# A graph kernel's edge sort moved from the front of the program into layer 1's blocks, as a check

## The chip, the cores and the metric

The kernel runs on one core of one Trainium2 chip. The metric is the device time in microseconds (us), the median of the runs. "PE" is TensorE, "DVE" VectorE, "ACT" ScalarE, "POOL" GpSimd, "SP" SyncE, which here only issues transfers.

## The reference

Two layers of a graph network over N = 6250 nodes and E = 206250 edges, width 64, all in float32. The edges are 100000 random pairs in both directions and a self-loop per node, sorted by `dst`.

```python
h = relu(layernorm(x))
# layer 0: edge (row, col) = (src, dst); 4 heads
e = concat(h[row], h[col])                            # 128 wide
a = pos[col] * exp(lrelu(lrelu(e @ gate_w1.T) @ gate_w2.T))
b = lrelu(lrelu(e @ msg_w1.T) @ msg_w2.T)
x = x + mean_heads(segment_sum(a * b, row) / segment_sum(a, row))
h = relu(layernorm(x))
# layer 1: gathers from src, sums at dst
m = (h[src] * sigmoid(feat @ prob_w.T)
     + (feat @ review_w.T) * sigmoid(feat @ score_w.T) * weight) * cj[src]
x = x + segment_sum(m, dst) * ci
```

Layer 0 sums at `src`, layer 1 at `dst`, while the input is sorted by `dst`.

## The kernel before

The edges stand in 403 blocks of 512 (4 tiles of 128), four blocks being a quad; the last one is partly padding. Both layers go block by block, and in both the sorted end of a block's edges lies in a narrow window of node numbers, so its rows come as a product with a 0/1 matrix, while the other end is gathered by indirect DMA.

The stages, in order of time:

- *Norm and tables* (VectorE L1189 to L1206). Then a loop over 49 columns of nodes builds `window_table`, the nodes' rows times the first weights in a high and a low part: PE `turn_column`, `project`, `project_rest`; ScalarE `copy_column`, `copy_high`, `copy_low` (L996 to L1016); GpSimd copies two small tail columns (L784); SP writes the rows out (L555, L558). After the loop ScalarE's queue issues the writes of `split_table`, the gather table of layer 0 (L1033, L1034), and the zeroing of the sums (L888).
- *The sort.* Layer 0 needs the edges by `src`. VectorE makes keys (`src` and `dst` packed in one positive float) and sorts all of them by a bitonic network: each of 128 partitions holds a run of 2048, a pass compares elements at a distance (`sort_pass`, L1429 and, for the passes after a turn, L1426), and between passes over runs and over partitions the array is transposed by PE in four PSUM banks (L1989), with ScalarE and VectorE moving two banks each (L1042, L1045, L1502, L1504). Then the sorted list is unpacked (`by_src`, `by_src_dst`, `by_src_first`), stored to DRAM, and each block's first node loaded back.
- *The verdict.* From the offsets of both lists a number `fits_sb` is made (L1566, L1569): 1 where each block's window is narrow enough. All engines load it (`fits`) and branch: `If` is the way with windows, `Else` a general way for any edge list, which isn't run with these inputs.
- *Layer 0* (`edges0_windows` on each engine, in loops of four blocks). SP loads a block's 32 rows of the window table (L535), the list's row (L540) and the gather's indices (`load_index`, L527). GpSimd gathers the far rows (L751, four a block) and adds the sums to DRAM (L765). PE is the busiest engine.
- *Between the layers* the sums are divided, added to `x`, normed again, and `src_table` is stored.
- *Layer 1* (`edges1_windows`, in loops of eight blocks). GpSimd gathers the `src` rows (L853, four a block, in four buffers; the gather of a block waits for the terms of the block four back). VectorE makes two dots (L1701, L1707), the 0/1 columns (L1733), and from the gathered rows the terms (L1737 to L1745). PE sums a quad in one bank (L2038), projects and adds it.

The order of the work is written out by hand for each engine; semaphores join them. In layer 1 of VectorE the part around the change is this:

```python
nc.vector.tensor_tensor(hot_four[m], columns_ps..., offset..., ALU.is_equal).then_inc(hot_ready, 1)   # L1733
dve.wait_ge(gates_ready, b + 1)
nc.vector.tensor_tensor(feat_gate_ps, gates_ps[:, 1, :], attn_quads[odd][:, m, :], ALU.mult)...       # L1737
dve.wait_ge(gathered1w[m], 64 * (quad + 1))
nc.vector.tensor_tensor(terms1_windows[m][:, :, 0:D], ends1_windows[m][:, :, 0:D], gates_ps...)       # L1739
```

Tiles whose names end in `_ps` are in PSUM.

## Time and profile before

| | us |
|---|---|
| median of 3 runs | 6826.49 (6826.26 to 6827.18) |
| span of the profiled execution | 5851.6 |
| its own time | not given beside the span |
| table build (36 to 176) | 140 |
| rest of the sort, verdict (176 to 522) | 346 |
| layer 0 (522 to 3795) | 3273 |
| between the layers (3795 to 3832) | 37 |
| layer 1 (3832 to 5852) | 2020 |

The span is the time from the first to the last instruction in the record; the median is 974.9 us longer. An engine's busy time counts its instructions, not its waits. A transfer stands in the record of the queue that issues it (SPq, ACTq) with the time of the issue alone, and as a share of the 16 DMA engines. The stretches' bounds are read off the timeline: the first window load of layer 0 and the first full blocks of layer 1.

### The profile page before, as it was taken

What the parts mean: (1) busy time and instruction counts of PE and PEld (TensorE: products, weight loads), DVE (VectorE), ACT (ScalarE), POOL (GpSimd) and SP (SyncE); (2) the same over time, 40 slices, a digit from 0 to 9 for tenths busy, and PEclk for the clock granted to TensorE, in tenths of its full rate; (3) what the DMA queues carried; (4) which work ended last, traced back from release to release, by engine and by line L of the source; (5) the groups of instructions that cost most, each with busy time, mean ns of one, the idle gap of its engine ahead of it and who ended that gap; (6) DMA issues with size and microseconds to landing.
All of it is one profiled execution on the core that took longest, in us unless ns stands there. A gap on an engine that the chain in (4) does not pass through costs nothing.

```text
span 5851.6 us, 116285 instructions
## 1 busy us (share of the span) xinstructions
PE 4355.2 (74%) x25010; PEld 2801.2 (48%) x25010; DVE 4656.5 (80%) x10137; ACT 2612.7 (45%) x6383; POOL 3496.4 (60%) x3689
## 2 busy tenths in 40 slices
PE   6214999999999999999999999545555555455455
PEld 4212555555555555555555555334444444444444
DVE  9887988989889898988989889756666666666665
ACT  5102777777777777777777777510000000000000
POOL 1002656666565665656656566367777777777776
PEclk9656999999999999999999999855555555555555
DMA  6601333333333333333333333333333323322332
GB/s 247 130 0 47 78 79 80 77 80 79 78 81 78 78 80 78 81 78 78 81 78 80 79 78 80 97 73 59 56 56 56 59 56 56 60 56 56 60 56 51
DMA packets 459109, 437.02 MB, mean 75 GB/s; under 512 B 268369, under 2 KB 340274, under 8 KB 457906
## 3 DMA queue, kind: packets, MB, share of 16 engines
q0 software_dynamic: 122512, 173.81, 18.0%
q1 hardware_dynamic: 308706, 249.41, 15.3%
q10 hardware_dynamic: 27840, 13.23, 1.4%
q8 instruction: 18, 0.29, 0.0%
q14 instruction: 33, 0.27, 0.0%
HBM read 363.27 MB, written 72.83 MB: 75 GB/s over the span
## 4 chain that ended last, share of the span: by engine, by line
PE 46%; POOL 17%; issue 13%; DVE 12%; DMA 6%; ACT 4%; ACTq 1%; SPq 0%; POOLq 0%; DVEq 0%
PE ps_hidden L1814 9%; POOL work L853 9%; PE ps_beta L1866 9%; POOL ends L853 8%; PE ps_hidden L1815 7%; PE ps_beta L1874 7%; DMA ends<-src_table,src_quads 5%; PE ps_alpha L1848 4%; DVE work L1429 4%; DVE work L1317 4%; PE ps_sum L1885 3%; ACT beta_scaled L949 3%; PE ps_T L1803 3%; PE ps_alpha L1857 2%; DVE work L1739 1%
## 5 line engine op out<-in xcount | busy, mean ns | idle before, releaser
L751 POOL DMA_INDIRECT ends<-split_table,src_pairs x1612 | 1581.0, 981 | 1571.7 <-issue 1435.0
L1317 DVE TENSOR_TENSOR work<-work,ps_hidden 128x512 f32<-128x512 f32 x1612 | 1102.3, 684 | 25.4 <-ACT work L897 6.5
L1814 PE MATMUL ps_hidden<-ends_parts,w_high 128*128 128x512 f32 x2418 | 1064.4, 440 | 60.5 <-DVE work L1317 58.8
L897 ACT ACTIVATE work<-ps_hidden 128x512 f32<-128x512 f32 x1612 | 960.6, 603 | 63.2 <-PE ps_hidden L1815 34.6
L1815 PE MATMUL ps_hidden<-ends_hot,window 128*128 128x512 f32 x2418 | 953.4, 394 | 0.0
L853 POOL DMA_INDIRECT work<-src_table,src_quads x808 | 764.4, 946 | 309.2 <-issue 222.0
L853 POOL DMA_INDIRECT ends<-src_table,src_quads x804 | 760.5, 946 | 245.2 <-issue 226.0
L2038 PE MATMUL ps_beta<-work,dst_rows_sb 128*128 128x128 f32 x1608 | 416.4, 441 | 565.6 <-DVE work L1745 565.6
L1115 ACT ACTIVATE ps_alpha<-dots 128x8 f32<-128x8 f32 x403 | 72.7, 180 | 1676.4 <-DVE dots L1707 1676.4
L1866 PE MATMUL ps_beta<-work,msg_w_sb 128*64 128x512 f32 x3224 | 804.1, 609 | 0.4 <-DVE work L1317 0.2
L2038 PE MATMUL ps_beta<-work,equal 128*128 128x128 f32 x1616 | 417.2, 440 | 509.1 <-DVE work L1745 509.1
L1322 DVE TENSOR_TENSOR beta<-beta_scaled,ps_beta 128x512 f32<-128x512 f32 x806 | 552.2, 685 | 288.1 <-ACT beta_scaled L949 280.3
L949 ACT ACTIVATE beta_scaled<-ps_beta 128x512 f32<-128x512 f32 x806 | 488.0, 605 | 562.1 <-PE ps_beta L1866 562.1
L1814 PEld LDWEIGHTS ps_hidden<-ends_parts,w_high 128*128 128x128 f32 x2418 | 454.6, 188 | 580.0 <-DVE work L1317 517.5
L2038 PEld LDWEIGHTS ps_beta<-work,dst_rows_sb 128*128 128x128 f32 x1608 | 358.1, 328 | 639.6 <-issue 611.1
L2038 PEld LDWEIGHTS ps_beta<-work,equal 128*128 128x128 f32 x1616 | 359.8, 328 | 556.1 <-issue 451.3
L897 ACT ACTIVATE scaled<-ps_hidden 128x512 f32<-128x512 f32 x806 | 489.6, 607 | 250.4 <-PE ps_hidden L1815 197.3
L1317 DVE TENSOR_TENSOR work<-scaled,ps_hidden 128x512 f32<-128x512 f32 x806 | 547.7, 679 | 2.3 <-ACT scaled L897 2.3
L1874 PE MATMUL ps_beta<-ident,beta 128*128 128x128 f32 x3224 | 506.4, 280 | 0.8 <-DVE beta L1322 0.7
L1815 PEld LDWEIGHTS ps_hidden<-ends_hot,window 128*128 128x128 f32 x2418 | 457.3, 189 | 56.2
L1874 PEld LDWEIGHTS ps_beta<-ident,beta 128*128 128x128 f32 x3224 | 357.1, 141 | 167.6 <-issue 165.6
L765 POOL DMA_DIRECT2D sums<-key_rows x403 | 371.3, 921 | 64.1 <-issue 28.4
(204 smaller groups left out, 6650.2 us busy)
## 6 DMA issues: line engine op xcount, KB each, us to landing
window<-window_table SPq DMA_DIRECT2D x403, 192.5 KB
parts<-in_edge_attr SPq DMA_DIRECT2D x101, 512.0 KB
dst_rows_sb<-by_src SPq DMA_DIRECT2D x403, 128.0 KB
ends<-split_table,src_pairs POOLq DMA_INDIRECT x1612
window_table<-parts SPq DMA_DIRECT2D x49, 386.0 KB, 2.4
sums<-key_rows POOLq DMA_DIRECT2D x403, 32.6 KB
work<-src_table,src_quads POOLq DMA_INDIRECT x808, 2.5
ends<-src_table,src_quads POOLq DMA_INDIRECT x804, 2.5
```

The lines of the kernel that those rows point to most:

```text
L751: pool.indirect_dma_start(out=ends[m][:, t, :], out_offset=None, in_=split_table, in_offset=bass.IndirectOffsetOnAxis(ap=src_pairs[m // 2] ...
L765: pool.dma_start(sums0[0][bass.ds(first, WIN0), :], quad_sum[m * WIN0:(m + 1) * WIN0, :], accum_op=ALU.add).then_inc(quad_added, 16)
L853: pool.indirect_dma_start(out=ends1_windows[m][:, t, :], out_offset=None, in_=src_table, in_offset=bass.IndirectOffsetOnAxis(ap=src_quads[ ...
L897: nc.scalar.activation(scaled[k % NL][:, :], ps_hidden[k % NL][:, :], ACT.Copy, scale=SLOPE).then_inc(scaled_ready, 1)
L949: nc.scalar.activation(beta_scaled[:, a * B:(a + 1) * B], ps_beta[a][:, :], ACT.Copy, scale=SLOPE).then_inc(beta_scaled_ready, 1)
L1317: nc.vector.tensor_tensor(hidden[k][:, :], scaled[k % NL][:, :], ps_hidden[k % NL][:, :], ALU.max).then_inc(hidden_ready, 1)
L1322: nc.vector.tensor_tensor(beta_T[a], beta_scaled[:, a * B:(a + 1) * B], ps_beta[a][:, :], ALU.max).then_inc(beta_ready, 1)
L1814: nc.tensor.matmul(o, w1_high[:, k * P:(k + 1) * P], ends_parts[j][:, :], start=True, stop=False)
L1815: nc.tensor.matmul(o, window[j][:, k * P:(k + 1) * P], ends_hot[j][:, :], start=False, stop=True).then_inc(hidden_done, 1)
L1866: last = nc.tensor.matmul(ps_beta[a][i * D:(i + 1) * D, :], msg_w2_sb[:, 2 * a + i, :], hidden[2 + 2 * a + i][:, :], start=True, stop=True)
L1874: last = nc.tensor.transpose(ps_beta[a][:, t * P:(t + 1) * P], beta_T[a][:, t * P:(t + 1) * P], ident[:, :])
L2038: last = nc.tensor.matmul(ps_beta[odd][0:WIN, 0:W1], hot_four[m][:, t, :], terms1_windows[m][:, t, :], start=(m == 0 and t == 0), stop=(m ...
```

## The change

Since the edges are given in both directions, the list by `src` is the list by `dst` with its ends swapped. Layer 0 now takes the input's list: `dst` as the sorted end where the sum goes, `src` as the gathered one. The exact check that this is right for the given edges is a sort of signed keys: an edge's key is its two ends packed (smaller first), with the sign of `src - dst`, 0 for self-loops and padding. The sorted keys, reversed and added to themselves, must be 0 everywhere. This sort runs in layer 1, from block 10 on, half a pass in a block of VectorE, half a turn in a block of PE and ScalarE. The verdict comes after layer 1. If it is 1 there is nothing more to do; `Else` starts again from `x` and computes both layers in the general way.

The core of the diff; `wait_more` and `begin_again` are of the `Else` way alone.

```diff
 # the plan, worked out while the program is built
+        def sort_plan():
+            halves, rounds, of, steps, moved, turn, b = {}, {}, 0, 1, 0, 0, SORT_FROM      # SORT_FROM = 10
+            def two_halves(d, run, turned, length):
+                for half in range(2):
+                    halves[b + half] = (of, d, run, turned, length, half, steps, moved)
+                return 1 - of, steps + (2 if run is None else 4), b + 2
+            for k in range(1, RUN_BITS + 1):                                               # RUN_BITS = 11
+                for i in range(k - 1, -1, -1):
+                    of, steps, b = two_halves(1 << i, (1 << k) if k < RUN_BITS else None, False, kept(1 << k))
+            for k in range(RUN_BITS + 1, SORT_BITS + 1):                                   # SORT_BITS = 18
+                for inward in (True, False):
+                    for r in range(2):
+                        rounds[b + r] = (turn, 2 * r, of, None if inward or k == SORT_BITS else k - RUN_BITS, steps)
+                    of, turn, moved, b = 1 - of, turn + 1, 4 * turn + 4, b + 2
+                    for i in range(k - RUN_BITS - 1, -1, -1) if inward else range(RUN_BITS - 1, -1, -1):
+                        run = (1 << (k - RUN_BITS)) if inward and k < SORT_BITS else None
+                        of, steps, b = two_halves(1 << i, run, inward and i == k - RUN_BITS - 1, RUN)
+            return halves, rounds, of, steps, turn, b
+        HALVES, ROUNDS, SORTED, SORT_STEPS, TURNS, MIRROR = sort_plan()
+        SETTLE = MIRROR + 6
 # VectorE
+            def sort_half(of, d, run, turned, length, half, steps, moved):
+                wait(dve, sort_moved, moved)
+                dve.wait_ge(sort_step, steps)
+                if run is None:       # one instruction of 1024 elements
+                    order_pairs(pairs(1 - of, d)[half], pairs(of, d), turned, (ALU.min, ALU.max)[half])
+                else:                 # two of 512
+                    out, given = pairs_of_way(1 - of, d, run, half, length), pairs_of_way(of, d, run, half, length)
+                    order_pairs(out[half], given, turned, ALU.min)
+                    order_pairs(out[1 - half], given, turned, ALU.max)
+            def check_part(b):
+                if SORT_FROM - 4 <= b < SORT_FROM:
+                    key_part(b - SORT_FROM + 4)      # one to four instructions of 1616 elements
+                if b in HALVES:
+                    sort_half(*HALVES[b])
+                if 0 <= b - MIRROR - 2 < 4:
+                    mirror_part(b - MIRROR - 2)      # 512 sums of a turned bank and the keys reversed
+                if 0 <= b - SETTLE < 8:
+                    settle_part(b - SETTLE)          # reach and mirror sums into fits_sb
             def edges1_windows(b, quad, half, m, odd):
...
                 nc.vector.tensor_tensor(hot_four[m], columns_ps...).then_inc(hot_ready, 1)
+                check_part(b)
                 dve.wait_ge(gates_ready, b + 1)
...
-            with dve.If(fit):
-                quads(dve, edges1_windows)
+            every_block(edges1_windows)             # written out; so are PE's and ScalarE's
+            fit = fits(dve)
+            with dve.If(fit):
+                settle(dve)
 # PE, ahead of a block's sums
+            def turn_round(n, i, of):
+                wait(pe, sort_moved, 4 * n + i)
+                for c in range(4):
+                    last = nc.tensor.transpose(turn_bank[:, c * P:(c + 1) * P],
+                                               runs[of][:, (4 * i + c) * P:(4 * i + c + 1) * P], ident[:, :])
+                last.then_inc(sort_turned, 1)
             def edges1_windows(b, quad, half, m, odd):
+                if b in ROUNDS:
+                    turn_rounds(*ROUNDS[b])          # two rounds
+                if 0 <= b - MIRROR < 6:
+                    mirror_rounds(b - MIRROR)
                 pe.wait_ge(terms1_step, 4 * b + 4)
 # ScalarE, behind a block's gates
+                if b in ROUNDS:
+                    move_rounds(*ROUNDS[b])          # each: wait sort_turned, copy the bank to the other run
 # ScalarE, start: the writes of the gather table ahead of the loop
             copy_high(0)
+            act.wait_ge(parts_split, 2)
+            act.wait_ge(step, STEPS_TABLE0)
+            act.dma_start(nodes(split_table)[:, :, 0:D], h_parts[0]).then_inc(tables_split, 16)
+            act.dma_start(nodes(split_table)[:, :, D:2 * D + 1], table_sb[:, :, :]).then_inc(tables_split, 16)
             for t in range(NT):
                 copy_low(t)
...
-            act.wait_ge(parts_split, 2)
-            act.wait_ge(step, STEPS_TABLE0)
-            act.dma_start(...)                       # the same two
             act.wait_ge(zeros_set, 1)
             zero_sums0(0, zeroed)
 # SP
             def load_index(b, a):
-                sp.dma_start(src_pairs[a][:, :], by_src_dst[:, bass.ds(b * T, 2 * T)]).then_inc(index_in[a], 16)
+                sp.dma_start(src_pairs[a][:, :].rearrange("p (b t) -> p b t", t=T),
+                             src[bass.ds(b, 2)].rearrange("b p t -> p b t")).then_inc(index_in[a], 16)
                 sp.dma_start(dst_rows_sb[j][D:P, :, :],
-                             by_src[bass.ds(b, 1)].broadcast_to([P - D, T, P])).then_inc(window_in[j], 16)
+                             dst_rows[bass.ds(b, 1)].broadcast_to([P - D, T, P])).then_inc(window_in[j], 16)
 # GpSimd
+            pool.wait_ge(tables_split, 32)
+            for b in range(3):
+                gather0_windows(b, 0, b)
+                gather0_tiles(b, T // 2)
+            pool.wait_ge(fits_step, 3)
+            pool.wait_ge(zeroed, 16 * 5)
+            fours(pool, edges0_windows)
 # VectorE during the table loop: the tail copies (GpSimd's before), the split of the far
 # weights, the offsets of both windows and their reach
+            for t in range(NT):
+                tail_rows(t)
+                if t == 1:
+                    split_far_weights()
...
```

After layer 0's sums are in, SP loads `src` and `dst` again for the keys, 1616 numbers a partition, behind the stores of `src_table`. The sort's two arrays now lie in `centered` and `table_sb`, the signs and the mirror's sums in `x_sb`.

## Rows read from the trace of the kernel before

**Rows 1.** The page: the span; busy us of each engine and share.

```profile
span 5851.6 us, 116285 instructions
PE 4355.2 (74%) x25010; PEld 2801.2 (48%) x25010; DVE 4656.5 (80%) x10137; ACT 2612.7 (45%) x6383; POOL 3496.4 (60%) x3689
```

**Rows 2.** By stretch: busy us of each engine, clock, DMA share, GB/s.

```profile
36.00:176.00 140.00, 118.75 (x687) 88.79 (x686) 137.85 (x230) 89.14 (x245) 20.18 (x47) 1.00 0.73 274
176.00:240.00 64.00, 7.32 (x32) 6.55 (x32) 45.93 (x42) 2.46 (x4) 0.00 (x0) 0.50 1.09 163
240.00:522.00 282.00, 49.77 (x211) 43.20 (x211) 247.76 (x280) 15.24 (x24) 0.00 (x0) 0.51 0.02 7
522.00:3795.00 3273.00, 3155.33 (x20150) 1795.31 (x20150) 2917.85 (x5693) 2355.50 (x5423) 1949.11 (x2015) 0.99 0.37 80
3795.00:3832.00 37.00, 1.56 (x7) 1.56 (x8) 21.23 (x49) 19.30 (x78) 8.33 (x9) 0.50 0.44 162
3832.00:5852.00 2020.00, 1021.12 (x3924) 865.30 (x3923) 1255.43 (x3815) 127.77 (x603) 1516.64 (x1604) 0.50 0.30 56
```

**Rows 3.** Groups of lines: busy us, mean ns, idle before; VectorE.

```profile
L1429 DVE TENSOR_TENSOR work<-work 128x512 f32<-128x512 f32 (+5 forms) x450 | 366.3, 868 | 5.8
```

**Rows 4.** Groups by form in layer 1, 4200 to 5600 us.

```profile
L853 POOL DMA_INDIRECT ends<-src_table,src_quads x560 | 529.7, 946 | 170.8 <-issue 158.3 <-DVE ps_sum L1742 6.4 <-DMA attn_quads<-in_edge_weight 4.9
L1739 DVE TENSOR_TENSOR work<-ends,ps_alpha 128x256 f32<-128x256 f32 x140 | 59.0, 421 | 251.0 <-DMA ends<-src_table,src_quads 251.0
L1739 DVE TENSOR_TENSOR work<-work,ps_alpha 128x256 f32<-128x256 f32 x140 | 59.0, 421 | 247.7 <-DMA work<-src_table,src_quads 247.7
```

**Rows 5.** Timeline, verdict to first block: start us, us, engine, line.

```profile
521.79 0.14 DVE L1569 TENSOR_SCALAR fits_sb<-reach 1x1 int32<-1x1 f32 x1
...
523.83 0.52 SPq L535 DMA_DIRECT2D window<-window_table  x1
...
527.99 0.49 DVE L1306 TENSOR_SCALAR ends_hot<-dst_rows_sb,window 64x512 fp32r<-64x512 int32 x1 [6.06 <-DMA dst_rows_sb<-by_src]
```

**Rows 6.** Timelines of SP's and ScalarE's queues, table's end.

```profile
175.73 0.33 SPq L558 DMA_DIRECT2D window_table<-parts  x1
...
175.25 0.62 ACTq L1033 DMA_DIRECT2D split_table<-parts  x1
...
175.90 13.64 ACTq L1034 DMA_DIRECT2D split_table<-table_sb  x1
189.59 23.96 ACTq L888 DMA_DIRECT2D sums<-parts  x5
```

**Rows 7.** By stretch, as rows 2, after the split_table issues.

```profile
189.60:218.00 28.40, 3.65 (x16) 3.27 (x16) 12.12 (x13) 1.09 (x2) 0.00 (x0) 0.50 1.29 95
218.00:232.00 14.00, 3.67 (x16) 3.27 (x16) 12.48 (x13) 1.37 (x2) 0.00 (x0) 0.50 0.99 413
```

**Rows 8.** Groups by form, 100 to 560 us: the sort.

```profile
L1429 DVE TENSOR_TENSOR work<-work 128x1024 f32<-128x1024 f32 x170 | 200.7, 1222 | 3.4
L1429 DVE TENSOR_TENSOR work<-work 128x512 f32<-128x512 f32 x168 | 105.0, 687 | 1.5
```

**Rows 9.** Timeline: a turn of the sort, three banks of four.

```profile
378.56 2.82 PE L1989 MATMUL ps_hidden<-ident,work 128*128 128x128 f32 x12 [27.26 <-DVE work L1429]
```

**Rows 10.** GpSimd's small copy: ns min/median/max, first and last start.

```profile
L784 POOL COPY parts<-tails x49: 188/418/694, 35.2 to 172.9; 128x4 f32<-128x4 f32 x49
```

**Rows 11.** Timelines of GpSimd and VectorE in layer 0, in order.

```profile
2000.51 1.05 POOL L751 DMA_INDIRECT ends<-split_table,src_pairs  x1 [0.30 <-issue]
...
2004.71 1.06 POOL L751 DMA_INDIRECT ends<-split_table,src_pairs  x1 [0.82 <-DVE parts L1330]
...
2005.00 0.28 DVE L1348 TENSOR_TENSOR equal<-columns,src_offset 128x128 fp32r<-128x128 f32 x1
...
2013.64 0.94 POOL L751 DMA_INDIRECT ends<-split_table,src_pairs  x1 [3.59 <-issue]
...
2013.98 0.28 DVE L1348 TENSOR_TENSOR equal<-columns,src_offset 128x128 fp32r<-128x128 f32 x1
```

More of the change, by code:

```diff
@@ L579, in _ @@
-            with sp.Else():
-                sp.wait_ge(lists_stored, 48)
-                blocks(sp, load0)
-                sp.wait_ge(zeroed1, 16 * T)
-            def read_sums0(c, copies):
-                if c >= 2 and copies == 1:
-                    sp.wait_ge(part_free, c - 1)
-                elif c >= 2:
-                    sp.wait_ge(x_summed, 2 * (c - 1))
-                for t in range(copies):
-                    sp.dma_start(parts[c % 2][:, t, :, :],
-                                 nodes(sums0[t][0:NP, :])[:, c * CH:(c + 1) * CH, :]).then_inc(part_in[c % 2], 16)
+            sp.wait_ge(fits_step, 3)
@@ L1390, in _ @@
-            for k in range(7):
-                nc.vector.tensor_scalar(lane[:, k:k + 1], lane[:, k:k + 1], k, 1, ALU.logical_shift_right,
-                                        ALU.bitwise_and).then_inc(signs_step, 1)
-            dve.wait_ge(signs_step, 7)
-            nc.vector.tensor_scalar(signs[:, 0:7], lane[:, 0:7], -2.0, 1.0, ALU.mult, ALU.add).then_inc(signs_step, 1)
-            keys = runs[1].bitcast(I32)
-            nc.vector.scalar_tensor_tensor(out=keys[:, 0:LIST], in0=runs[0][:, 0:LIST].bitcast(I32), scalar=FIELD,
-                                           in1=keys[:, 0:LIST], op0=ALU.logical_shift_left,
-                                           op1=ALU.bitwise_or).then_inc(key_step, 1)
@@ L1441, in offsets_of_targets, with tail_rows, split_far_weights @@
-            def offsets_of_targets():
+            dve.wait_ge(tail_step, 2)
+            def tail_rows(t):
+                if t >= 2:
+                    dve.wait_ge(row_out[t % 2], 16 * (t // 2))
+                nc.vector.tensor_copy(low_row[t % 2].rearrange("p (a w) -> p a w", a=2)[:, :, 0:2],
+                                      tails[:, t, :, :]).then_inc(tail_ready, 1)
+            def split_far_weights():
+                dve.wait_ge(w_high_ready, 1)
+                for j in range(2):
+                    nc.vector.tensor_tensor(window[j][0:D, 0:HID], w1_far[0:D, :], w1_high[0:D, :].bitcast(F32),
+                                            ALU.subtract).then_inc(w_low_ready, 1)
@@ new lines, in signs_of_lanes, with offsets_of_quads @@
+            def signs_of_lanes():
+                dve.wait_ge(lanes_ready, 1)
+                for k in range(7):
+                    nc.vector.tensor_scalar(lane[:, k:k + 1], lane[:, k:k + 1], k, 1, ALU.logical_shift_right,
+                                            ALU.bitwise_and).then_inc(signs_step, 1)
+                dve.wait_ge(signs_step, 7)
+                nc.vector.tensor_scalar(signs[:, 0:7], lane[:, 0:7], -2.0, 1.0, ALU.mult, ALU.add).then_inc(signs_step, 1)
+            def offsets_of_quads():
@@ L1509, in _ @@
-            for k in range(1, RUN_BITS + 1):
-                for i in range(k - 1, -1, -1):
-                    at = sort_pass(at, 1 << i, (1 << k) if k < RUN_BITS else None, length=kept(1 << k))
-            for n, (k, inward, _, _) in enumerate(TURNS[:-1]):
-                at = turn_runs(n, k, inward, at)
-                for i in passes(k, inward):
-                    run = (1 << (k - RUN_BITS)) if inward and k < SORT_BITS else None
-                    at = sort_pass(at, 1 << i, run, turned=inward and i == k - RUN_BITS - 1)
@@ L2078, in project_sums @@
                 last.then_inc(review_done, 1)
+            fit = fits(pe)
             with pe.If(fit):
-                quads(pe, edges1_windows)
-                turn_window(NQ - 1)
-                project_window(NQ - 1)
+                settle(pe)
             with pe.Else():
+                begin_again(pe)
+                transpose_ends(0, 0, 0)
+                blocks(pe, edges0)
+                for t in range(T):
+                    sum_tile(NB - 1, t, 1)
                 blocks(pe, edges1)
```

1039 lines of the change are left out of this document (520 added, 519 removed).

## The prediction

> **What bounds the kernel now.** I read the busy table first, then a table by stretches, then in each stretch the groups of lines and a timeline, always with one question: which engine never waits here.
>
> The span is 5851.6 us [rows 1]. The page gives no other time of the profiled execution; the median of the runs is 6826.5, so 974.9 us lie around the span. Nothing in the trace shows what they are. I hold them fixed: every sum below is taken from the span and carried over as it stands.
>
> The stretches are the key [rows 2]. From 36 to 176 us the window table is built: PE and ACT work, the DMA share is 0.73, VectorE is busy 138 of 140 us, but with the sort, not with the table. From 176 to 522 only VectorE works: PE is busy 57 of 346 us and GpSimd not at all. The sort's line L1429 has 450 instructions of 366.3 us [rows 3]. This part is serial: nothing of layer 0 starts before the sorted list. Layer 0 (522 to 3795) has PE busy 3155 of 3273 us at clock 0.99, 8.1 us for each of 403 blocks. Layer 1 (3832 to 5852) is different: PE 1021, VectorE 1255 and GpSimd 1517 of 2020 us, 5.0 us a block. There the gathers bound it: each takes 0.946 us, 170.8 us of idle time stand before 560 of them, 0.30 us each, put down to issue [rows 4], so four of them make 4 x 1.25 = 5.0. VectorE in layer 1 waits for gathered rows: 251.0 + 247.7 us before L1739 in 280 blocks, 1.78 us a block [rows 4].
>
> So the change takes work from where it is alone and puts it where its engine waits 1.78 us in every 5.0.
>
> **What is removed.** Layer 0's first instruction that waits for the list is the match at 527.99, 6.2 us after the verdict at 521.79 [rows 5]. Now it waits for the window table alone, which has its last transfer issued at 175.7 [rows 6]. Three terms stand between 175.7 and the new start.
>
> 1. ScalarE's queue now issues the two split_table transfers ahead of the table loop. Before they took 0.62 and 13.64 us of that queue, after it [rows 6]. They stand in ScalarE's order ahead of its copies of the table rows, so the loop starts late. ScalarE had a pause of about 1 us there and PE starts some 3 us earlier, since the one-row product now comes behind the first projection: 14.3 - 4 = 10 us. Last issue at 186.
> 2. When the second issue is done, the transfer is not: DMA stayed busy at 1.29 for 28.4 us more [rows 7]. Now this meets the table's own writes at 0.73 of the engines [rows 2]. Bounds: 0 if it fits in the idle share, 28 if it comes in series. I take the middle, 14: 0.27 of 140 us is 38 us of free share, enough on paper, but small and large packets take turns. Last issue at 200.
> 3. Landing 2.5, and from window load to match 4.2 as before [rows 5]. The zeroing of sums0, formerly under the sort, now runs against these first loads; before, its five issues took 24 us, mostly behind the split writes, and then 14 us at 0.99 DMA share [rows 6, 7]. I add 2 (bounds 0 and 6). GpSimd waits for the zeroing before block 3's gathers; the first three blocks' gathers are already made during the build, and they give PE 24 us of work, so that wait is covered. If the cover failed it would cost 10 to 15 us.
>
> Start at 209, bounds 193 and 227. Saved: 528 - 209 = **319 us**, bounds 301 to 335.
>
> The fields, block ends, by_src stores and the lists' loads back (508 to 522) are inside that number. Table tails move from GpSimd to VectorE: 49 small copies on an engine now idle there, nothing. The offset lines, the lane signs and the weight split go between them, hidden by the 2.8 us that each table row takes. Layer 0's body is the same instructions on all engines; load_index reads 16-byte pieces (256 of them) instead of 32-byte ones (128), on SP's queue, which has 8.1 us a block for three or four issues: nothing, at most some us. The stage between the layers is the same.
>
> **What is added to layer 1.** The plan has 66 passes inside runs of 2048, 28 inward and 77 outward ones: 171 passes, two blocks each, 342 blocks; and 14 turns of two blocks, 28. It starts at block 10, so the mirror comes at 380, the verdict is read after block 402. 95 passes (190 blocks) put one 1024-element instruction into a block, 76 passes (152 blocks) two of 512. Price: 1.22 us for 1024 elements and 0.69 for 512, of which about 0.63 is left when they follow each other [rows 8]. So 1.22 to 1.3 us a block, against 1.78 of waiting: it fits, with 0.5 over. It is put between the hot columns (L1733) and L1737, just ahead of the wait for rows, so it fills that wait. Key parts (blocks 6 to 9) cost up to 4 us in a block: lag of 4 to 5 us, which four gather buffers (a gather waits for the terms of four blocks back, 10 us or more of reserve) absorb and the 0.5 us over gives back.
>
> Turn blocks: four transposes are about 0.9 to 1.06 us (12 in 2.82) [rows 9], ScalarE's move 0.6 to 0.7; one bank now, so strictly in turn, 2.1 us a round with the handovers, 4.2 a block. Queued behind them are, on PE, the block's sums (2.1 us) and the quad's projection; on ScalarE the next block's gates. PE then needs 6.3 us a block for two blocks, ScalarE's gates come up to 1.3 us late, once, and VectorE has no sort in these blocks. VectorE waits only for sums three blocks back. I take +3 us for all 14 turns and the mirror, bounds 0 and 60 (2 us for each of 28 + 6 blocks, were nothing absorbed). Plus 2 at the end for reading the verdict. The loops of PE, ScalarE and VectorE are written out; the sort itself was straight code and L1429 sat idle 5.8 us before 450 instructions [rows 3]: nothing.
>
> **The unknown: does the sort slow the gathers?** Every VectorE instruction of layer 1 before has one operand in PSUM or one tensor only; the sort's have two inputs in SBUF. The trace shows such an overlap in two places. GpSimd's small copy L784, made during the sort, takes 188 ns at best, 418 in the median and 694 at worst [rows 10]: it waits out part of a sort instruction. A gather is another thing: in layer 0 L1348 (two SBUF inputs, 0.28 us) began 0.34 us into the gather of 2013.64, which took 0.94 like its neighbours; and 0.29 us into that of 2004.71, which took 1.06, as the gather of 2000.51 did with no L1348 in it [rows 11]. So between 0.3 and 0.6 us a gather needs nothing of what VectorE holds. Its first 0.3 us and its last third are not shown. From this I take 0 as the value, nearest to the rows on gathers, and keep both other ends.
>
> The Trainium skill ("SBUF — State Buffer", Who interferes with whom) says that a VectorE instruction with two SBUF inputs contends with a GpSimd instruction that reads SBUF, and the second to issue is blocked until the first ends; L784's rows agree. It also infers that descriptor generation needs the write interface, which tensor_tensor leaves alone; the rows on L1348 fit that. A gather does read its 128 indices from SBUF, so by the first rule it is held at one moment: the first rival.
>
> **Forecast.** 6826.5 - 319 + 3 + 2 = **6512 us**, own range 6490 to 6560.
>
> **Rivals.**
> - *Each gather is held once, at its start.* For: L784; the untested first 0.3 us. Against: nothing measured. A sort instruction of 1024 elements reads for about 1.1 us; gathers start every 1.25, so it catches one with 0.88 and holds it 0.55 on average: 0.48 x 190 = 92 us. Two of 512: 2 x 0.44 x 0.275 = 0.24, x 152 = 37. Together 129: 6641 us.
> - *A gather stands still whenever VectorE reads twice.* Against: [rows 11]. A gather is running 0.946 / 1.25 = 76% of the time: 342 x 1.1 x 0.76 = 286: 6798 us.
> - *Slower: sort and gathers exclude each other wholly in layer 1*, queue gaps included, so GpSimd's 5.0 us a block becomes 5.0 + 1.24: 342 x 1.24 = 424, less 319, plus 5: 6937 us. It decides from 319 / 342 = 0.93 us lost per sort block. For: a GpSimd instruction was held 0.5 us by a 0.63 us one. Against: [rows 11] and VectorE's own L1348, which keeps 0.28 with a gather in flight.
> - *The check doesn't pass* and both layers run again the old general way: over 10,000 us (more than twice layer 0's 3273). The input is built from (s, d), (d, s) and self-loops, so it is symmetric, and self-loops and padding get key 0.
> - *Lags add up* (turns, key parts): +60, 6570 us.
>
> **Chances.** Forecast 44; lags 4; held once 27; held throughout 11; near no change 3; slower by exclusion 9; check fails 2. Two runs of this kernel differ by up to 0.01%; I call 0.2% (14 us) the least that tells from no change. Faster: 44 + 4 + 27 + 11 = 0.86; same 0.03; slower 0.11. The range goes from 6480 (start at 193 and a little more from layer 0) to 6720: it holds the forecast, the lags, the first rival with its own spread of 60 us and the lower edge of the second.
>
> **What would show it.** The first match at 200 to 220 us instead of 528; layer 0 as long as before (3273), PE clock 0.99 there. In layer 1 the row of L853: mean 946 ns and 5.0 us a block if I am right; a mean of 1.02 to 1.05 us, with some gathers 0.3 to 1.0 us longer, for the first rival; about 1.12 for the second. VectorE's wait before L1739 falls from 1.78 to about 0.5 us. ScalarE's split_table issues at 37 to 51 us. The prediction is wrong if layer 1's stretch grows by more than 50 us, if the table build ends after 230, or if the time around the span is not 975 again.

## The result, and the profile after

The changed kernel takes 6369.7 us (median of 4 runs, 6355.6 to 6388.4), the kernel before beside it 6826.8: ratio 0.9331, 95% interval 0.9309 to 0.9352. That is 457 us faster, where I had forecast 314, and 110 us below the low end of my range.

The page of the changed kernel, first its span and busy times; they answer to [rows 1].

```profile
span 6380.7 us, 112465 instructions
PE 4448.9 (70%) x25026; PEld 2772.9 (43%) x25026; DVE 4638.8 (73%) x10169; ACT 2628.9 (41%) x6414; POOL 3558.8 (56%) x3640
```

This span agrees with the time of its run (6382.3) within 2 us. The one before did not, 5851.6 against 6826 [rows 1], so the first thing to settle was the old trace. The kernel before, run again with a profile (the first experiment), has a span of 6816.8 us for a time of 6818.5. By stretch, with the columns of [rows 2]: the kernel before, run again, layer 0 and layer 1,

```profile
530.00:3970.00 3440.00, 3240.34 (x20143) 1778.28 (x20142) 2877.58 (x5647) 2338.58 (x5339) 1942.94 (x2007) 1.00 0.33 74
4033.00:6812.00 2779.00, 1020.05 (x3923) 864.76 (x3922) 1260.61 (x3814) 127.86 (x604) 1516.81 (x1604) 0.50 0.21 41
```

and the changed kernel, the table's build, layer 0 and layer 1:

```profile
36.00:215.00 179.00, 132.60 (x680) 97.93 (x678) 22.65 (x78) 89.78 (x243) 11.52 (x12) 0.90 0.86 235
...
240.00:3650.00 3410.00, 3243.13 (x20137) 1769.52 (x20135) 2876.95 (x5644) 2332.50 (x5336) 1932.69 (x2000) 1.00 0.35 75
...
3715.00:6374.00 2659.00, 1064.08 (x4182) 899.19 (x4182) 1661.74 (x4334) 161.04 (x663) 1600.91 (x1604) 0.51 0.23 43
```

Against [rows 2] the reader sees: the busy times of layer 1 in the kernel before are the same in both of its profiles (VectorE 1255 and 1261, GpSimd 1517 and 1517), but it lasts 2020 us in the first and 2779 in the second. Nothing lies around the span: the spans of the two profiles differ by 965 us, and these are idle time inside, 764 in layer 1 (6.95 us a block instead of 5.00) and 200 in layer 0 (8.46 instead of 7.97).

One sentence that all numbers below need: in some comparisons the kernel before takes 5844 to 5849 us and in others 6824 to 6827, each within 0.1%, and TensorE's granted clock in layer 0 is 0.99 to 1.00 in both; the first trace is of the former kind and the timing of the change of the latter, so each experiment is read only against the kernel before beside it. I call them the 5844 and the 6826 comparisons.

What differs between them is SyncE. The instructions of one line of its layer 1 loop (the row window's second load; minimum, median and maximum ns, then first and last start), the first trace and the kernel before run again:

```profile
L653 SPq ALU_OP  x85: 32/37/37, 4011.7 to 5692.8; - x85
L653 SPq MOVE ci_windows<-in_node_vec_n x85: 29/29/29, 4011.7 to 5692.9; - x85
```

```profile
L653 SPq ALU_OP  x86: 13/701/1411, 4223.4 to 6588.9; - x86
L653 SPq MOVE ci_windows<-in_node_vec_n x86: 4/699/737, 4223.4 to 6589.6; - x86
```

The register move of this line has a median of 29 ns in one and of 699 in the other; the issue of the load behind it goes from 346 to 700. In the 6826 profile of before, counted over layer 1 (4033 to 6812 us): of SyncE's register and branch instructions begun within 4 us after a gather's start 552 of 1055 take over 600 ns, of those begun later 0 of 209; in layer 0 (530 to 3970) it is 242 of 2945 within 2.5 us and 0 of 538 later. In the first trace it is 0 of 4770. Only SyncE is slow: no such instruction of ScalarE, VectorE or GpSimd takes over 600 ns in either profile (ScalarE's 102 register moves of layer 1 have a median of 29 ns in both). And this divides all the traces: over the whole program the seven of 6826 comparisons have 241 to 794 of over 600 ns, the thirteen of 5844 comparisons, the first trace among them, have none.

This is what GpSimd waits for in the kernel before, run again, 4700 to 6100 us (against [rows 4], where the DMA part is 4.9 us in 1400):

```profile
L853 POOL DMA_INDIRECT ends<-src_table,src_quads x403 | 381.2, 946 | 122.9 <-issue 122.9
L853 POOL DMA_INDIRECT work<-src_table,src_quads x400 | 378.3, 946 | 512.6 <-DMA attn_quads<-in_edge_weight 398.9 <-issue 106.7 <-DVE ps_sum L1737 7.0
```

The gathers themselves take 946 ns in both. They stop once in each quad of four blocks because the loads of the next quad, its indices among them, come late (the row names the last of the three loads that share a semaphore). Means over 80 quads, us after the quad's first gather, worked out from the traces:

```
kernel, comparison        window load  next quad's load  next first gather
before, 5844 (rows 4)          9.7           11.1              20.0
before, 6826                  12.8           22.7              27.8
changed, 6826                 14.1           20.0              26.4
changed without sort, 6826    12.1           22.2              27.7
```

### The profile page after: what moved, and what is told of

It reads as the page before. It is cut to its first block, busy times and chain, and to the rows that moved or that the text cites. A ratio compares the mean times of both kernels' runs of the same rounds, so it can differ in the third digit from the quotient of the medians.

```text
span 6380.7 us, 112465 instructions
## 1 busy us (share of the span) xinstructions
PE 4448.9 (70%) x25026; PEld 2772.9 (43%) x25026; DVE 4638.8 (73%) x10169; ACT 2628.9 (41%) x6414; POOL 3558.8 (56%) x3640
## 4 chain that ended last, share of the span: by engine, by line
PE 39%; issue 25%; DVE 10%; POOL 6%; SPq 6%; DMA 5%; ACT 4%; another core or an unknown queue 4%; DVEq 1%; ACTq 0%; POOLq 0%
PE ps_beta L1922 12%; PE ps_hidden L1870 8%; PE ps_hidden L1871 7%; POOL work L827 4%; DVE work L1358 3%; PE ps_sum L1941 3%; POOL ends L827 3%; PE ps_beta L1930 3%; PE ps_alpha L1904 1%; DMA attn_quads<-in_edge_weight 1%; SPq L592 1%; DMA ends<-src_table,src_quads 1%; PE ps_alpha L1913 1%; ACT beta_scaled L969 1%
## 5 line engine op out<-in xcount | busy, mean ns | idle before, releaser
L827 POOL DMA_INDIRECT work<-src_table,src_quads x808 | 806.8, 998 | 856.4 <-DMA attn_quads<-in_edge_weight 361.8
L1870 PE MATMUL ps_hidden<-ends_parts,w_high 128*128 128x512 f32 x2418 | 1097.4, 454 | 159.2 <-ACT ends_hot L964 60.0
L911 ACT ACTIVATE work<-ps_hidden 128x512 f32<-128x512 f32 x1612 | 947.2, 600 | 219.3 <-PE ps_hidden L1871 179.6
L827 POOL DMA_INDIRECT ends<-src_table,src_quads x804 | 802.7, 998 | 257.9 <-issue 244.1
L1922 PE MATMUL ps_beta<-work,msg_w_sb 128*64 128x512 f32 x3224 | 827.6, 611 | 4.6 <-issue 0.9
```

Source lines behind the costliest of these rows:

```text
L827: pool.indirect_dma_start(out=ends1_windows[m][:, t, :], out_offset=None, in_=src_table, in_offset=bass.IndirectOffsetOnAxis(ap=src_quads[ ...
L911: nc.scalar.activation(scaled[k % NL][:, :], ps_hidden[k % NL][:, :], ACT.Copy, scale=SLOPE).then_inc(scaled_ready, 1)
L1870: nc.tensor.matmul(o, w1_high[:, k * P:(k + 1) * P], ends_parts[j][:, :], start=True, stop=False)
L1922: last = nc.tensor.matmul(ps_beta[a][i * D:(i + 1) * D, :], msg_w2_sb[:, 2 * a + i, :], hidden[2 + 2 * a + i][:, :], start=True, stop=True)
```

## The experiments

**The kernel before once more.** No edit.

> The kernel before, unchanged, once more, with a profile of its own. The first trace of it has a span of 5851.6 us while its timed runs are 6826 us, and none of SyncE's small instructions in it takes over 0.6 us; in the changed kernel a span agrees with its time within 3 us, and over 500 of SyncE's in layer 1 take 0.7 us each. Theory A (the first trace was of an execution that lacked something that the timed ones have): a span of about 6825 us, with layer 0 at about 8.4 us a block or layer 1 at about 6.6 instead of 8.0 and 5.0, and SyncE's small instructions at 0.7 us in it. Theory B (a fixed part lies outside the span of this kernel): a span of 5852 us again, 975 us around it.

Measured: 6824.6 us, span 6816.8. Theory A holds; its rows are above.

**The sort taken out, loops as they are, loops as loops, and SyncE written out.** In the first, the turns of TensorE and ScalarE are out too, and check_part keeps one line:

```
-                if b in HALVES:
-                    sort_half(*HALVES[b])
...
+                if b == SETTLE + 7:
+                    nc.vector.memset(fits_sb[:, :], 1).then_inc(fits_ready, 1)
```

> The changed kernel without the check's work in layer 1: no key parts, no sort halves, no turns, no mirror, a verdict of one written as a constant; the loads of the lists stay, and the three loops stay written out. Its answer to whether the list is symmetric is left out. Changed kernel: layer 1 at 6.62 us a block, 6370 us in all. If the sort is what layer 1 pays for: 5.0 us a block, about 5730 us. If SyncE's slow instructions (0.7 us each, index loads 7 to 8 us late in every quad of blocks) are, and they have nothing to do with the sort: 6.3 to 6.7 us a block, 6250 to 6370 us.

The second has quads(pe, ...), quads(act, ...) and quads(dve, ...) for every_block(...) besides.

> As the kernel without the check's work, with the layer 1 loops of TensorE, ScalarE and VectorE as loops again instead of written out. If the written-out code of three engines, fetched all through layer 1, is what slows SyncE: 5.0 us a block here, about 5730 us, against 6.3 to 6.7 with it written out. If SyncE's slowness has another cause (where its own code lies): the same 6.3 to 6.7 us a block in both.

The third is the changed kernel with one line:

```
-            quads(sp, load1_windows)
+            every_block(load1_windows)
```

> The changed kernel, sort and all, with SyncE's layer 1 loop written out like the other engines'. If SyncE's loop pays 0.7 us an instruction because it jumps back to code that has to be fetched anew: straight code has none of it, index loads come in time, layer 1 at 5.0 to 5.3 us a block, 5730 to 5860 us. If all of SyncE's instructions are slow there whatever the loop: 6.6 us a block again, 6370 us. If the sort is the cause: 6370 us.

Measured, before at 6826.3: 6483.9, 6495.7 and 6452.9 us. Three things fall. Without the sort layer 1 is not faster but slower, 6.94 us a block against 6.60; so the sort is not what it pays for. Written-out code of three engines isn't what slows SyncE either: with their loops back the kernel takes 12 us more, and 553 of SyncE's instructions in layer 1 are slow instead of 566. And SyncE without a loop, though it runs 508 such instructions there instead of 1277, still has 92 of over 600 ns (459 in the changed kernel) and is 83 us slower than the changed kernel. This last one is no clean test of the late load: from 4500 to 6000 us GpSimd waits 209 us for VectorE's terms and 119 us for the load, and VectorE up to 19 us at a time for ScalarE's gates.

**SyncE's order.** If the late load is the bound, it must pay to issue it ahead of the row window of the quad before, which waits until that quad's second block:

```
                     load1_quad(quad, odd)
-                    sp.wait_ge(out_ready, quad - 1)
-                    settle(sp)
-                if m == 0:
-                    load_x_window(quad, odd)
+                    if not (isinstance(quad, int) and quad == 2):
+                        sp.wait_ge(out_ready, quad - 2)
+                        settle(sp)
+                if m == 0 and not (isinstance(quad, int) and quad == 0):
+                    load_x_window(quad - 1, 1 - odd)
...                                              # the last quad's row window, behind the loop
```

> The kernel before, with one change of order on SyncE in layer 1: the index, attribute and weight loads of a quad are issued ahead of the row window of the quad before it, no longer behind it. Theory S (layer 1 at 6.95 us a block is the index load that comes late, since SyncE needs 13 us for 17 small instructions while gathers are in flight and the load waits behind the window's): the load is issued some 8 us earlier, the gathers no longer wait 8.9 us in each quad, layer 1 at 5.0 to 5.3 us a block, 6040 to 6170 us in all. Rival (the gathers themselves or the load's own DMA are slow in the timed runs): no gain, 6750 to 6830 us.

> The changed kernel with the same change of order on SyncE. Theory S: 6.62 us a block falls to 5.2 to 5.5 (a gather takes 1.004 us on average with the sort, 0.944 without, so four of them make 5.24, and VectorE's turns add some), 5800 to 5920 us. If it is the sort on VectorE that layer 1 waits for: 6.2 to 6.6 us a block, above 6200 us.

> The changed kernel without the check's work in layer 1 and with the same change of order on SyncE. Theory S: 5.0 to 5.1 us a block, 5700 to 5770 us; and the sort then costs what it adds, 60 to 150 us over this one in the kernel with the sort and the new order, where with SyncE's old order the sort made layer 1 114 us shorter. Rival (the written-out code of TensorE and ScalarE, which stalls some 9 us at a time, bounds layer 1 too): 5.4 to 6.0 us a block, 5860 to 6100 us.

> The changed kernel with each of layer 1's gathers replaced by a plain load of 128 rows of the table by GpSimd's queue, as many bytes into the same tiles; the rows chosen by the edges are left out of the output's layer 1. If a gather in flight (its list of 128 addresses, made and run) is what makes SyncE's instructions take 0.7 us: none of them is slow in layer 1, all the slow ones of layer 0 stay, and layer 1 is at 4.2 to 5.2 us a block. If any traffic of GpSimd's queue, or anything else of the stage, does it: over half of them stay slow and layer 1 at 6 us a block or more.

This fell into a 5844 comparison (before 5844.3): 5844.6, 5668.3, 5527.4 and 5221.4 us. Where SyncE is not slow its order is worth nothing in the kernel before, and the question on the late load stayed open. The last kernel, with a plain load for each gather, could not show whether gathers are what slows SyncE, since nothing does there; it shows layer 1 without gathers at 4.2 us a block, VectorE busy 1606 of 1680 us: the bound behind the gathers is VectorE with the sort in it.

**Both kernels in one 5844 comparison.**

> The changed kernel, unchanged, beside the kernel before. The kernel before took 6826 us where the changed one was timed, and 5844 us in the last comparison, where none of SyncE's small instructions took 0.7 us. Where before takes 5844: theory (the early start of layer 0 gives 317 us, the sort takes 129 to 141 back by holding gathers at their start) says 5660 to 5680 us, a ratio of 0.969 to 0.972, whatever SyncE's order. Where before takes 6826: 6370 us again. Rival (the two parts differ by chip alone and the change gains 7% everywhere): 5450 us where before takes 5844.

Measured: 5615.9 us against 5844.1, ratio 0.9609 (0.9581 to 0.9637). Beside it the kernels of the new order again: before 5844.1, changed 5665.5, without the sort 5524.1. Over that last kernel the sort costs 92 us in SyncE's old order and 141 in the new one. (The kernel without the sort was run at 5844 in the new order alone; that the order is worth nothing without a sort is read off the kernel before.) So in the changed kernel the early load costs 50 us here.

**SyncE slowed on purpose.** 18 register loads ahead of each row window, in the old order as shown and in the new order, where the same lines stand ahead of `load_x_window(quad - 1, 1 - odd)`:

```
+                    if not first_quads(quad):
+                        for _ in range(DELAYS):      # 18
+                            window_start(sp, 4 * quad)
                     load_x_window(quad, odd)
```

> The kernel before with 18 extra register loads on SyncE (0.65 us each by the trace, 11.7 us) ahead of each row window of layer 1, and so ahead of the index load that is issued behind it. Where the kernel before takes 5844 us: Theory S (a load that leaves 11.7 us later makes each quad wait 7 to 8 us, as where SyncE is slow by itself) says 27 to 28 us a quad instead of 20, 6.8 to 7.0 us a block, 6560 to 6660 us. Rival (SyncE has 10 us or more to spare, and what makes layer 1 slow elsewhere is something else): 5844 to 5900 us. Where before takes 6826: 7500 us or more under S.

> The same 18 register loads ahead of each row window, in the kernel before with the loads of a quad issued ahead of the window of the quad before. Where the kernel before takes 5844 us: Theory S says 5840 to 5880 us, since the load leaves before the extra work and SyncE needs 15 of 20 us a quad; if SyncE's extra work costs wherever it stands, 6500 us or more. Where before takes 6826: SyncE needs over 25 us a quad and no theory is told apart by it.

Measured, before at 5849.2: 6498.1 and 5849.4 us. The same extra work costs 649 us ahead of the load and nothing behind it. The row window leaves 10.1 us later than in [rows 4]'s trace (19.8 against 9.7 us after the first gather) and the next first gather 6.6 (26.6 against 20.0): the load had 3.5 us to spare. GpSimd's rows of the two, 4000 us to 6400 and to 5700:

```profile
L857 POOL DMA_INDIRECT work<-src_table,src_quads x724 | 682.9, 943 | 814.0 <-DMA attn_quads<-in_edge_weight 610.3 <-issue 190.9 <-DVE ps_sum L1741 12.8
```

```profile
L860 POOL DMA_INDIRECT work<-src_table,src_quads x682 | 644.1, 944 | 207.8 <-issue 180.3 <-DVE work L1752 25.3 <-DMA attn_quads<-in_edge_weight 2.1
```

So a load 10.1 us late makes each quad 6.6 us longer, with the same releaser in the same row; in the 6826 comparison it is 11.6 us late and the quad 7.8 us longer. That is layer 1 of the kernel before. The kernel before with the early load and no extra work, run beside them and expected at 5844 or at 6040 to 6170, took 5849.3; it never met a 6826 comparison.

**The sort behind the arrival of the rows.** What the sort costs in the 5844 comparisons is read off gathers. Two blocks of the changed kernel there, GpSimd's gathers and VectorE's sort (L1647):

```profile
4601.24 1.22 DVE L1647 TENSOR_TENSOR table_sb<-centered 128x1024 f32<-128x1024 f32 x1
4601.77 1.50 POOL L827 DMA_INDIRECT ends<-src_table,src_quads  x1 [0.30 <-issue]
...
4606.07 0.94 POOL L827 DMA_INDIRECT ends<-src_table,src_quads  x1 [0.30 <-issue]
4606.41 1.22 DVE L1647 TENSOR_TENSOR table_sb<-centered 128x1024 f32<-128x1024 f32 x1
4607.32 1.12 POOL L827 DMA_INDIRECT work<-src_table,src_quads  x1 [0.31 <-issue]
```

The gather of 4601.77 starts with 0.69 us of a sort instruction left and takes 0.56 more than 0.94. That of 4606.07 has one begin 0.34 into it and takes 0.94. That of 4607.32 starts with 0.31 left and takes 0.18 more. Over all of layer 1, worked out from the trace (this kernel, 5844 comparison):

```
sort instruction at the gather's start      gathers   longer by, mean ns
under 0.1 us left                               23       -1
none, or one begins later in the gather       1285        8 (median 0)
under way, 0.1 to 0.2 us left                   47       29
under way, 0.3 to 0.4 us left                   56      218
under way, 0.5 to 0.6 us left                   45      413
under way, 1.0 to 1.2 us left                    9      987
(the classes between are left out)
in all: 327 gathers start under a sort instruction, 82.4 us
```

So a gather is held once, at its start, by what is left less 0.1 us. The edge is sharp: in this trace the seven gathers that start at most 15 ns after a sort instruction are not held (in the kernel with the sort behind the rows it is so up to 42 ns), the next three, at 24 to 30 ns, are held for 0.53 us, and the 306 into which one begins take 944 ns in the mean. Two kernels put the sort where it begins just behind a gather's start, one with SyncE's order too; the second product with the gates moves ahead of the sort with it:

```
-                check_part(b)
                 dve.wait_ge(gates_ready, b + 1)
...
                 dve.wait_ge(gathered1w[m], 64 * (quad + 1))
+                dve.wait_ge(terms1_step, 4 * b + 1)
+                nc.vector.tensor_tensor(feat_gate_ps.unsqueeze(2), feat_gate_ps.unsqueeze(2),
+                                        ends1_windows[m][:, :, D:D + 1], ALU.mult).then_inc(terms1_step, 1)
+                check_part(b)
...                                              # the product's old place, three lines down, is empty
```

> The changed kernel with the check's work moved within VectorE's block: from ahead of the wait for the gathered rows to just behind it, after the 0.17 us product of the gates (which now comes first). Rows land 3.9 us after their gather's start, so that wait ends 0 to 0.1 us after the start of the third gather behind it; a 1.22 us sort instruction then starts 0.15 to 0.35 us into one gather and is over 0.1 to 0.3 us after the next one's start. Theory H (a gather is held only if a sort instruction is under way when it starts, by what is left of it less 0.1 us): the held time falls from 82 us to 15 to 40, layer 1 at 5.03 to 5.12 us a block, 5550 to 5600 us where the kernel before takes 5844 and the changed one 5616. Rival (the hold goes by the time that the sort instructions take, wherever they stand, or VectorE's later terms now hold the gathers up): 5616 us or more. Where before takes 6826: 6370 us or somewhat more, since the late load bounds layer 1.

> The same, with SyncE's loads of a quad ahead of the row window of the quad before. Where the kernel before takes 5844 us: the same 5550 to 5600 us under Theory H. Where it takes 6826: Theory S (late load) says layer 1 at 5.0 to 5.3 us a block in place of 6.6, 5700 to 5850 us; if the late load is not the bound there, 6300 us or more.

Measured, before at 6824.4: 6517.4 and 6236.7 us. The held time in the first is 8.6 us against 82.7 in the changed kernel's trace, as Theory H says; yet it is 148 us slower than the changed kernel: at 7.02 us a block it waits for the late load, which leaves 22.5 us after the quad's first gather. The early load takes 281 us off (ratio of the second to before 0.9138, 0.912 to 0.9156), but 6236.7 is far from the 5700 to 5850 that I expected. Its profile was taken at a mean granted clock of 0.68 where its timed runs have 0.79; the difference is in layer 0 (0.81 against 1.00 in the kernel without the early load), while layer 1 has 0.51 in both, so of layer 1 the waits are read. It has the load's wait gone, and others in its place; the waits of GpSimd and of VectorE, 4500 to 6000 us (total, times, longest):

```profile
POOL work L830 <- DVE work L1788: 228.7, 86, 9.0
...
POOL ends L830 <- DMA attn_quads<-in_edge_weight: 1.2, 4, 0.3
```

```profile
DVE ps_sum L1779 <- ACT ps_alpha L1135: 214.9, 29, 18.3
DVE parts L1758 <- remote: 136.9, 22, 11.6
```

("Remote" is a releaser that the profile cannot name.) GpSimd now waits for VectorE's terms, VectorE for gates that ScalarE makes up to 18 us late, 29 times. What stalls there is open. ScalarE's code is written out, but it is so in the kernel without the sort too, and there VectorE has no wait for gates between 4500 and 6000 us in a 6826 comparison; code that is written out is not enough by itself.

> The changed kernel with the check's work just behind the arrival of the gathered rows, and SyncE's loads of a quad ahead of the window of the one before. Where the kernel before takes 5844 us: Theory H (a gather is held only if a sort instruction is under way when it starts) says 10 to 40 us held in all, layer 1 at 5.03 to 5.12 us a block, 5550 to 5600 us, against 5616 of the changed kernel and 5668 with SyncE's order alone. Rival (the hold goes by the time that the sort takes, wherever it stands): 5616 to 5670 us. Where before takes 6826: 6235 us again, with ScalarE's stalls in its written-out code as the longest wait of VectorE.

Measured: 5600.4 us against 5845.0, ratio 0.9584 (0.9568 to 0.9600). It is 65 us below the same order without the move, at the very end of what I expected. It is 16 below the changed kernel, but these two stand in different comparisons, and the intervals of their ratios touch (0.9581 and 0.9600). 67.1 us are held, not 10 to 40: of 419 sort instructions between 3600 and 5300 us only 152 begin in the first 0.2 us after a gather's start. But time follows the held sum:

```
5844 comparisons           held under   all gathers longer   layer 1 over that     time, us
                           a sort, us   than 944 ns each, us  without sort, us
changed                      82.4             92.6                 93              5615.9
changed, early load         129.7            140.9                141              5668.3
sort behind rows, early      67.1             74.1                 75              5600.4
```

What the sort costs layer 1 is what its gathers are longer, to 1 us in each of the three. The last kernel is the shortest complete one measured in either kind of comparison (5600 and 6237); the changed kernel with the early load alone was never met by a 6826 comparison.

## Why the prediction was wrong

- **The time around the span, "I hold them fixed": the step that failed.** There is no such time. The trace that I worked from has no register instruction of SyncE in layer 1 that takes over 0.6 us, the timed runs have hundreds near 0.7 us, and layer 1 was bound there by an index load that left 11.6 us later than in [rows 4]'s trace, not by the gathers. A sum made on 5.0 us a block and carried over to 6826 could be right only by chance. And the 975 us did not stay: of the 143 us by which the change gained more than forecast, 114 are the difference between the kernel with the sort and without it, in a layer that waits for the late load; 23 are what the start and layer 0 gave beyond 319; 5 were set aside for turns and verdict.
- **The start of layer 0.** ScalarE's queue, the last table issue, the first window load and the first match of the changed kernel in the 5844 comparison, columns as in [rows 5]:

```profile
36.79 12.11 ACTq L1047 DMA_DIRECT2D split_table<-table_sb  x1
...
200.80 0.33 SPq L574 DMA_DIRECT2D window_table<-parts  x1
...
210.49 0.52 SPq L551 DMA_DIRECT2D window<-window_table  x1
...
220.84 0.49 DVE L1347 TENSOR_SCALAR ends_hot<-dst_rows_sb,window 64x512 fp32r<-64x512 int32 x1 [22.69 <-DMA dst_rows_sb<-in_dst_rows]
```

  The last table issue, forecast at 200, is at 200.8 in the 5844 comparison and 215.4 in the 6826. The terms of 10 and 14 have the right sum there, but not as two effects spread over the build: the table's rows are 8 us behind at the first, 25 by the seventh, and no more up to the 49th (in the 6826 comparison 40 by the tenth). The first match, forecast at 209 in bounds of 193 to 227, is at 220.8, for the third term was too small: 20.0 us instead of 8.7. The window load leaves 9.7 us after the last issue, not 2.5, and the match comes 10.3 us after the load, not 4.2 + 2; all this while the DMA share is 0.99 to 1.03, with the zeroing issued at 200.3 to 204.9. In the 6826 comparison the match is at 235.3, against 523.5 before. In time the kernels without the sort are 317 and 320 us below before at 5844, for a forecast of 319: of the 317, 305 are the start (528.0 to 222.8 in that kernel) and 13 layer 0's blocks at 7.93 instead of 7.97 us. At 6826 it is 342; the profiles give 289 for the start and 41 for layer 0 (8.46 us a block before, 8.39 without the sort).
- **The sort fits into VectorE's wait: right.** The wait for rows, by form, of the changed kernel in the 5844 comparison, 3900 to 5300 us:

```profile
L1779 DVE TENSOR_TENSOR work<-ends,ps_alpha 128x256 f32<-128x256 f32 x134 | 56.4, 421 | 132.4 <-DMA ends<-src_table,src_quads 132.2
L1779 DVE TENSOR_TENSOR work<-work,ps_alpha 128x256 f32<-128x256 f32 x133 | 56.0, 421 | 131.5 <-DMA work<-src_table,src_quads 131.5
```

  It falls from 1.78 us a block [rows 4] to 0.99 (263.9 in 267 blocks; I said 0.5): VectorE still waits for gathers, 245 times in these 267 blocks, with the sort in them.
- **"From this I take 0 as the value": the second step that failed**, at 5844 by 92 us. The rows on which I leaned [rows 11] show an instruction that begins inside a gather, and such a one indeed does nothing; the untested first 0.3 us was the place. The first rival, *held once at its start*, had the mechanism, and its size was 129 us, where 82 are held in the changed kernel (129.7 with the early load, which is how gathers and sort happen to fall, not what I reckoned). The mean gather of layer 1 takes 1.001 us; I had said 0.946, and 1.02 to 1.05 for this rival. Layer 1's stretch grew from 2020 to 2104 us at 5844, over the 50 that I had named as a sign of being wrong. The Trainium skill ("SBUF — State Buffer", Who interferes with whom) says that the one of the two that issues second is blocked until the first ends; the table of held gathers agrees. The other way round these runs show no blocking: a sort instruction of 1024 elements that begins inside a gather takes 1.216 us in the mean of 177, one that does not 1.220 (11). I gave this 27%.
- **Turns and key parts, 3 us: too low, but small.** At 5844 the 28 turn blocks cost 4.5 us in all, the four key parts 5.4, the mirror and the verdict 0.4, together 10.3; the 342 sort blocks cost the other 82.5 of the 93.
- **The sign of the sort in the 6826 comparisons** was in none of my cases: with it layer 1 takes 2659 us, without it 2778. The load leaves 2.2 us earlier in the mean of quads, unevenly (quads of 20.6 to 39.5 us, where without the sort they take 24.0 to 29.0), and only if the sort stands ahead of the wait for rows: behind it, 7.02 us a block. Why is not settled. With the sort ahead 459 of SyncE's register and branch instructions in layer 1 are slow, without it 566, with it behind the rows 488. Gathers that pause in mid-quad and so leave SyncE alone are not the reason: over 0.6 us between two gathers of a quad is found in 5 of 80 quads with the sort and in 6 without.

In sum, by comparison: at 5844 the change is worth 228 us (forecast 314, first rival 185), at 6826 it is worth 457, of which 342 are the start and layer 0 and 114 the sort's unforeseen effect on a layer that waits for SyncE. My range failed on the latter: without the 114 the time would have been 6484, just inside its low end.

**Open:** what makes SyncE's instructions slow in some comparisons. It is not one chip against another, if the record's numbers of the chips are taken as they stand: two comparisons ten minutes apart bear the same number and have before at 5849.2 and 6824.4. That the slowness goes with gathers in flight is shown by when the long instructions occur, not by an experiment. That it bounds layer 1 through the late load is shown by the slowed kernels at 5844, and in one kernel, that with the sort behind the rows, by the early load's 281 us at 6826, which leaves over half of layer 1's loss to other waits; for the kernel before it was not tried at 6826. Open too is why the sort shortens layer 1 there.

## What to carry to other kernels

Compare the profiled execution's span with the timed runs before anything else. Where a profile was taken of a timed run here, the two agreed within 3 us; a difference of 975 us meant a trace of another regime, and no term read from it could be carried over as fixed. Look at what feeds the bound engine for its spare time, not only at the bound engine: here a load with 3.5 us to spare sat behind one that waits for the previous quad's rows. Moving it ahead cost nothing in the kernel before, and 50 us at 5844 in the changed one, where more gathers then started under a sort instruction. Where VectorE's instructions with two SBUF inputs stand beside GpSimd's gathers, count which gathers start under one; the price is what is left of it then.

## What the hardware showed that I had not expected

The same register move of SyncE had a median of 29 ns in one execution and 699 in another of the same kernel. The slow instructions of layer 1 lie near 0.7 us or near 1.4, all within 4 us after a gather's start; the other engines' register instructions kept their times, and so did the gathers with 946 ns. And a gather of 944 ns started under a sort instruction with 0.69 us left took 1.50 us, while one into which such an instruction began at 0.34 us took 0.94.
